# Wide attention: each tile's values weighted by products of 64 rows in two halves of the array

## The reference

```python
qh = (q_in @ wq + bq).reshape(b, q_len, H, K)      # H = 16 heads, K = 128
kh = (kv_in @ wk + bk).reshape(b, t, H, K)
vh = (kv_in @ wv + bv).reshape(b, t, H, K)
kh = jnp.concatenate([kh, jnp.broadcast_to(bias_k, (b, 1, H, K))], axis=1)
vh = jnp.concatenate([vh, jnp.broadcast_to(bias_v, (b, 1, H, K))], axis=1)
logits = jnp.einsum('bqhk,bthk->bhqt', qh, kh) / scale
weights = jax.nn.softmax(logits, axis=-1)
ctx = jnp.einsum('bhqt,bthk->bqhk', weights, vh).reshape(b, q_len, H * K)
return ctx @ wo + bo
```

## Time and profile before

| | us |
|---|---|
| median of three runs | 1942.26 (1941.73 to 1946.75) |
| the profiled execution | 1941.19 |
| its span, from first to last instruction | 1939.5 |
| PE busy | 1731.0 (89%) |
| PEld busy | 1470.4 (76%) |
| DVE busy | 1002.6 (52%) |
| ACT busy | 998.8 (51%) |
| POOL busy | 431.9 (22%) |
| mean granted TensorE clock | 0.942 of full speed |

### The profile page before, as it was taken

The page is one execution under the profiler, slowest core; times in us unless marked ns, Lnnn a source line. Parts: engine busy times, 40 slices in busy tenths (PEclk is TensorE's granted clock), DMA queues, the critical chain, the costliest instruction groups (busy, mean ns, idle before and its releaser), DMA issues. The chain is left out here.

```text
span 1939.5 us, 36373 instructions
## 1 busy us (share of the span) xinstructions
PE 1731.0 (89%) x14350; PEld 1470.4 (76%) x14350; DVE 1002.6 (52%) x2150; ACT 998.8 (51%) x1890; POOL 431.9 (22%) x399
## 2 busy tenths in 40 slices
PE   5999999999979999999998598899489689699597
PEld 4888889888858888898887488577366467567486
DVE  6444444444364444444443733677678566667633
ACT  4545555455435555555554344566457476476443
POOL 5000000000020000000000300345510377377400
PEclk7999999999979999999999799899789799799799
DMA  4000000000020000000000100000100000100101
GB/s 153 23 22 22 0 22 22 22 22 0 1 67 23 22 22 0 22 22 22 22 0 1 47 0 8 21 2 2 52 1 0 26 2 2 36 2 2 47 0 44
DMA packets 55049, 39.77 MB, mean 21 GB/s; under 512 B 11891, under 2 KB 54451, under 8 KB 54963
## 3 DMA queue, kind: packets, MB, share of 16 engines
q1 hardware_dynamic: 54962, 38.57, 6.7%
HBM read 36.46 MB, written 2.10 MB: 20 GB/s over the span
## 5 line engine op out<-in xcount | busy, mean ns | idle before, releaser
L689 DVE TENSOR_TENSOR l0a_c_lo<-l0a_c_ps,l0a_c_hi 128x512 fp32r<-128x512 f32 x128 | 88.6, 692 | 267.2 <-ACT l0a_c_hi L643 267.2
L631 ACT ACTIVATE l0a_weight_t<-l0a_t_ps 64x256 f32<-64x256 f32 x256 | 96.8, 378 | 230.7 <-PE l0a_t_ps L532 229.2
L728 DVE TENSOR_TENSOR x<-l0a_o_ps,x 128x1024 f32<-128x1024 f32 x64 | 78.4, 1225 | 202.9 <-PE l0a_o_ps L102 202.9
L552 PEld LDWEIGHTS l0a_c_ps<-l0a_weight_t,l0a_v 128*128 128x128 f32 x1024 | 135.3, 193 | 14.4 <-ACT l0a_weight_t L631 3.0
L100 PE MATMUL l0a_o_ps<-l0a_wo_hi,l0a_c_hi 128*128 128x256 f32 x512 | 144.2, 282 | 0.0
L101 PE MATMUL l0a_o_ps<-l0a_wo_lo,l0a_c_hi 128*128 128x256 f32 x512 | 143.8, 281 | 0.0
L102 PE MATMUL l0a_o_ps<-l0a_wo_hi,l0a_c_lo 128*128 128x256 f32 x512 | 143.7, 281 | 0.0
L102 PE MATMUL l0a_v_ps<-l0a_wv_hi,ctx_lo 128*128 128x256 f32 x512 | 143.6, 280 | 0.0
L100 PE MATMUL l0a_v_ps<-l0a_wv_hi,ctx_hi 128*128 128x256 f32 x512 | 143.6, 280 | 0.0
L101 PE MATMUL l0a_v_ps<-l0a_wv_lo,ctx_hi 128*128 128x256 f32 x512 | 143.0, 279 | 0.0
L552 PE MATMUL l0a_c_ps<-l0a_weight_t,l0a_v 128*128 128x128 f32 x1024 | 136.9, 277 | 1.7 <-ACT l0a_weight_t L631 1.7
(11 more groups left out here) (426 smaller groups left out, 4877.5 us busy)
## 6 DMA issues: line engine op xcount, KB each, us to landing
l0a_raw<-in_L_xattn_wq_dram SPq DMA_DIRECT2D x32, 128.0 KB, 2.3
l0a_raw<-in_L_xattn_wk_dram SPq DMA_DIRECT2D x32, 128.0 KB, 2.3
l0a_raw_v<-in_L_xattn_wv_dram SPq DMA_DIRECT2D x16, 256.0 KB, 3.3
l0a_raw_o<-in_L_xattn_wo_dram SPq DMA_DIRECT2D x32, 128.0 KB, 2.8
l0a_wo_all<-in_L_xattn_wo_dram SPq DMA_DIRECT2D x2, 2048.0 KB, 8.3
ctx_rows<-in_ctx_dram SPq DMA_DIRECT2D x4, 512.0 KB, 5.7
x<-in_x_dram SPq DMA_DIRECT2D x4, 512.0 KB, 8.9
l0m_raw<-in_L_xattn_w_fc_dram SPq DMA_DIRECT2D x2, 1024.0 KB, 5.5
```

The source lines that it names most:

```text
L552: last = pe.matmul(by_tile[:, m, b, :, :], v[(j - HP) // HP % 2][:, m * HB + b, p * K:(p + 1) * K], weight_t[:, m, b, :, :].rearrange("p a ...
L631: last = act.activation(weight_t[half, :, :, a, :], t_ps[half, 0:GT // 2 * P] .rearrange("p (m b q) -> p m b q", b=HB, q=SEQ), ACT.Copy)
L689: dve.tensor_tensor(c[p][1][:], c_ps[:], c[p][0][:].bitcast(F32), ALU.subtract).then_inc(c_lo, 1)
L728: dve.tensor_tensor(chip.x[:, rows, :], o_ps[:], chip.x[:, rows, :], ALU.add).then_inc(added, 1)
```

## The change

The array is used in two halves of 64 rows. For each (m, b) and each half a, a product of 64 rows weights the values in half a of the value tile by the 64 columns of the weights in the same half, and writes 64 columns of c. So `weight_t` has no blocks for the other half and no zeros, one copy of 128 partitions fills it, and the memset, the semaphore `zero_done` and ScalarE's wait for it are gone. The two halves write to different PSUM banks: `tc_ps` is two banks, of which the first holds t in its left half and c of a = 0 in its right half, and the second c of a = 1 in its right half. ScalarE's and VectorE's instructions on c read those two quarters and write `c` in the order it had. The waits that order t and c are the ones of before.

```diff
-            weight_t = sb("weight_t", [P, GT // 2, HB, 2, SEQ])
+            weight_t = sb("weight_t", [P, GT // 2, HB, SEQ])
+            HALF_GN = GN // 2
             c = [split(f"c{p}", [P, GN]) for p in range(HP)]
-            q_ps, k_ps, v_ps, s_ps, t_ps, c_ps = (
-                chip.ps(f"{tag}_{x}_ps", [P, GN], stack) for x in ("q", "k", "v", "s", "t", "c"))
+            q_ps, k_ps, v_ps, s_ps = (
+                chip.ps(f"{tag}_{x}_ps", [P, GN], stack) for x in ("q", "k", "v", "s"))
+            tc_ps = chip.ps(f"{tag}_tc_ps", [P, 2, 2, HALF_GN], stack)
+            t_ps = tc_ps[:, 0, 0, :]
+
+            def c_of(t):
+                return t.rearrange("p (m a n) -> p a m n", a=2, n=P)
+            c_ps = tc_ps[:, :, 1, :].rearrange("p a (m n) -> p a m n", n=P)
...
-            zero_done = chip.sem(f"{tag}_zero_done")
...
-                    pool.memset(weight_t[:], 0.0).then_inc(zero_done, 1)
                     passes(pool, slots)
...
-                            by_tile = c_ps[:].rearrange("p (m a b q) -> p m b a q", a=2, b=HB, q=SEQ)
                             for m in range(GT // 2):
                                 for b in range(HB):
-                                    last = pe.matmul(by_tile[:, m, b, :, :], v[(j - HP) // HP % 2][:, m * HB + b, p * K:(p + 1) * K],
-                                                     weight_t[:, m, b, :, :].rearrange("p a q -> p (a q)"), start=True, stop=True)
+                                    for a in range(2):
+                                        half = slice(a * SEQ, (a + 1) * SEQ)
+                                        last = pe.matmul(c_ps[:, a, m, b * SEQ:(b + 1) * SEQ],
+                                                         v[(j - HP) // HP % 2][half, m * HB + b, p * K:(p + 1) * K],
+                                                         weight_t[half, m, b, :], start=True, stop=True)
                             last.then_inc(c_made, 1)
...
-                            for a in range(2):
-                                half = slice(a * SEQ, (a + 1) * SEQ)
-                                last = act.activation(weight_t[half, :, :, a, :], t_ps[half, 0:GT // 2 * P]
-                                                      .rearrange("p (m b q) -> p m b q", b=HB, q=SEQ), ACT.Copy)
-                            last.then_inc(t_done, 1)
+                            act.activation(weight_t[:].rearrange("p m b q -> p (m b q)"), t_ps, ACT.Copy).then_inc(t_done, 1)
...
-                            act.activation(c[p][0][:], c_ps[:], ACT.Copy).then_inc(c_hi, 1)
+                            act.activation(c_of(c[p][0][:]), c_ps, ACT.Copy).then_inc(c_hi, 1)
...
-                    act.wait_ge(zero_done, 1)
                     passes(act, slots)
...
-                            dve.tensor_tensor(c[p][1][:], c_ps[:], c[p][0][:].bitcast(F32), ALU.subtract).then_inc(c_lo, 1)
+                            dve.tensor_tensor(c_of(c[p][1][:]), c_ps, c_of(c[p][0][:]).bitcast(F32), ALU.subtract).then_inc(c_lo, 1)
```

## The result

The kernel after the change takes 1983.23 us (median of 4 runs, 1982.08 to 1985.52) against 1941.99 us for the kernel before in the same comparison (4 runs): a ratio of 1.0215, 95% interval 1.0198 to 1.0233. It is slower by 41 us. The profiled execution took 1982.08 us, its span 1980.4 us at a mean granted clock of 0.944 (before: 1939.5 us at 0.942).

A forecast was written before the change was run, and what follows sets the result against it. TensorE's sequence was taken to bound the wide attention. 124 slots at +0.34 us (+42.2 us) less 1.5 us in the tail slots gave +40.7 us, 1983.0 us against the median of 1942.26; range 1965 to 1998 us.

The forecast's parts named there:

- TensorE's sequence is the time: In the wide attention's steady stretch TensorE is busy 458.21 of 460 us, so time added to its sequence shows in the span.
- Entry, 0.31 plus an uncovered load of 0.11: Switch into c's 64-row form: 0.31 us from q's last product to c's first load, then that load uncovered, 0.11 us.
- Eight steps of 0.111, the halves side by side: Inside c's block, eight pairs of loads at 0.111 us each, loads setting the pace; the other half adds 0.01 us.
- Exit, 0.15: Switch out of c's 64-row form: 0.15 us from c's last product to k's first load.
- The sum, 0.34 us a slot: From q's last product to k's first load, 1.36 us instead of 1.01; taken as 0.34 in 124 slots, 42.2 us.
- Tail, -1.5 us: In the four tail slots TensorE waits for ScalarE's weights copy; one copy instead of two saves up to 1.5 us.
- Copy at 378 ns, c_hi and c_lo at no more, zero fill at nothing: ScalarE's one weights copy at 378 ns, saving 0.38 us; c_hi, c_lo at 597 and 692 ns; dropped zero fill worth nothing.
- Rival A: Halved products halve c's block: steps of 0.06 us, 0.95 us from q's last product to k's first load; 1932 us, 4%.
- B: No cost at switches of form: only the tail's gain, -1.5 us, 1941 us (5%); one side free, 1962 us (3%).
- C: The halves of c's block take turns: 16 steps of 0.111 us instead of 8, +153 us, 2094 us; 5%.
- D: New gaps lower the granted clock: a tenth of such slots' work at half speed, 96 us more, 2079 us; 3%.

The follow-up runs named there:

- early: On the kernel before, ScalarE makes the next pass's w_hi ahead of its copy of k: 1934.02 us; the same on quad: 1922.20 us.
- one half: The changed kernel without the products of the upper half, eight loads and eight products in a slot, results not the program's: 1985.10 us.
- narrow: The changed kernel with each of c's products streaming 32 columns instead of 64, results not the program's: 1982.15 us.
- quad: The changed kernel with c's products cut into quadrants of 64 by 64 and the block's waits ahead of q's last product: 1928.84 us.
- split: The changed kernel with c's sixteen products issued in two blocks of eight, the second in the middle of k: 2023.62 us.
- outer: The changed kernel with all eight products of the lower half ahead of those of the upper half in program order: 2045.18 us.

## Why the prediction was right

Predicted were 1983.0 us and slower with 90%; measured were 1983.23 us.

- *TensorE's sequence is the time.* Right: 0.333 us a slot came out as 40.5 us in the two stretches, and what was taken from TensorE's waits elsewhere (early) came out whole as well.
- *Entry, 0.31 plus an uncovered load of 0.11.* The first load came 0.32 after q's last product.
- *Eight steps of 0.111, the halves side by side.* Right; one half and narrow show that loads set them and that the second half adds 0.01.
- *Exit, 0.15.* Off: it was 0.20. I had taken the recorded start of the last product as the start of its stream. In this form it is written 0.056 us after the start of a load that takes 0.111, so some 0.05 before the load is done (in narrow, with 32 columns, 0.028 us after the load's start). By the same reading my 0.11 + 0.78 + 0.01 to the last product's start was 0.06 too long (0.84). The two errors cancel, since they are one: the time was counted on the wrong side of the last product. Quad, with loads of 64 columns, has 0.15 at its exit. Counted from the end of the last load (0.78 + 0.11), the stream of 0.05 and the exit leave 0.09 of drain in the kernel after, drain being the time from the end of the last stream to the next form's first load. In quad (0.42 + 0.06, 0.05) it is 0.09 too, and in narrow (0.78 + 0.11, 0.03) as well.
- *The sum, 0.34 us a slot.* Measured 0.348 to k's first load, 0.333 over the whole slot; where the 0.015 between them goes wasn't traced. The rows had given 0.35, and I took 0.34 because the step looked a little under 0.111. It was 0.112, so that reason failed, though the slot as a whole came out nearer to 0.34.
- *Tail, -1.5 us.* Some 0.9: the first tail slot gained 0.38, the second only 0.08, because less of a wait was left there to gain from. The term was mis-sized by 0.6 us. With these small errors, and runs of one kernel 3.4 us apart, that forecast and median lie 0.2 us apart is luck; the mechanism and a size within 1 or 2 us are not.
- *Copy at 378 ns, c_hi and c_lo at no more, zero fill at nothing.* 385 ns; c_hi 598 and c_lo 691 ns. In the second attention the value products begin 14.56 us after the stage's first transposes before and 14.57 after, and q follows them without a gap in both, so nothing is to be seen of the fill.
- *Rival A* (a step of 0.07 or less) fell with its reason: the 0.06 comes back in quad, because the loads' columns are halved there, and A's 0.95 us from q's last product to k's first load is what quad took (0.944). *B* fell to split. *C* fell for the order used; outer is a partial case of it. (The pairs that the prediction holds against C are those of the earlier trace rows, not rows 6.) *D*: the clock stayed at 1.00 and 0.99 in the steady stretches.

## What to carry to other kernels

Before a product is cut to fewer rows, read from its neighbours in TensorE's order whether they keep the form of the array: each visit to the 64-row form cost 0.33 to 0.35 us here, so work in that form is to be gathered into one visit, or be long. Inside it the columns of weights of each load set the pace, so cut those (quadrants halved the block) and alternate the halves product by product. When a reordering takes time off the bounding engine, look at once at what was just in time before: here 12.6 of the 18 us came back as waits at 14 places.

## What the runs showed of the hardware that was not expected

- In a 64-row block the last product's recorded start lies 0.056 us after its load's start, whether the load takes 0.111 us or 0.06, so the exit reads 0.20 us behind loads of 128 columns and 0.15 behind loads of 64, with the same drain of 0.09.
- The halves pair only when their passes stand near each other in the program: 0.97 us for the 16 loads in turn, 1.47 with one half's eight first.
- Dropping half of the products (one half) or half of their columns (narrow) didn't change the block by more than 0.03 us.
- A 0.42 us operation of VectorE with both inputs in SBUF took 1.45 us beside POOL's split of a weight tile; one with an input in PSUM kept its 0.43 there.
